# Cross-attention and expert FFN on one core: set-up reordered, last pair's sums ahead of the gathers, rows spread by transposes

## What is computed

```python
x = x + xattn(layernorm(x), ctx, q_w, k_w, norm_w, gate_w, gate_b)   # 16 sequences of 128 tokens, 256 wide
x = x + ffn(layernorm(x), combine_weights, top_idx, W1, b1, W2, b2)  # 8 experts, 512 rows each

def xattn(h, mem):
    n = rmsnorm(h) * norm_w
    v = concat(n, mem)
    a = softmax(mask((n @ q_w.T) @ (v @ k_w.T).T / 16))
    g = sigmoid(h @ gate_w.T + gate_b)
    return (1 - g) * h + g * (a @ v)

def ffn(x):       # expert e: rows tok = top_idx[:, e]
    y = gelu(x[tok] @ W1[e] + b1[e]) @ W2[e] + b2[e]
    out[tok] += y * combine_weights[tok, e]
```

## Time and profile before

| | us |
|---|---|
| median of 3 runs (275.99 to 277.49) | 276.33 |
| the profiled execution | 277.63 |
| its span, first to last instruction | 275.8 |
| PE, DVE, ACT, POOL busy, share of the span | 96%, 79%, 68%, 57% |

### The profile page before, as it was taken

The page is one execution under the profiler, slowest core; times in us unless marked ns, Lnnn a source line. Parts: engine busy times, 40 slices in busy tenths (PEclk is TensorE's granted clock), DMA queues, the critical chain, the costliest instruction groups (busy, mean ns, idle before and its releaser), DMA issues.

```text
span 275.8 us, 5127 instructions
## 1 busy us (share of the span) xinstructions
PE 265.7 (96%) x1474; PEld 226.7 (82%) x1474; DVE 219.0 (79%) x554; ACT 188.2 (68%) x349; POOL 155.9 (57%) x153
## 2 busy tenths in 40 slices
PE   6999999999989999999999999999999999999992
PEld 2688899999866888888888888888888888888992
DVE  1788999898986499968878896796887889689452
ACT  2488898887575976685677587658657758763540
POOL 4283865655843956556446466655645646605515
PEclk9799999999999999999999999999999999999998
DMA  7993247568454956455565544546555461201211
GB/s 219 358 263 94 77 123 218 155 214 276 114 182 123 350 160 157 124 192 167 138 195 163 154 139 135 157 122 209 156 138 189 156 175 53 67 26 47 62 38 69
DMA packets 30292, 42.44 MB, mean 154 GB/s; under 512 B 5251, under 2 KB 24015, under 8 KB 30148
## 3 DMA queue, kind: packets, MB, share of 16 engines
q1 hardware_dynamic: 25392, 30.00, 34.4%
q0 software_dynamic: 4608, 12.24, 15.4%
q10 hardware_dynamic: 276, 0.00, 0.1%
HBM read 33.54 MB, written 9.24 MB: 155 GB/s over the span
## 4 chain that ended last, share of the span: by engine, by line
PE 83%; DVE 6%; issue 4%; POOL 3%; ACT 2%; DMA 1%; DVEq 0%; POOLq 0%; ACTq 0%
PE bank L1398 19%; PE bank L1185 13%; PE bank L1186 12%; PE bank L1187 12%; PE bank L1399 10%; PE bank L1229 4%; PE bank L1274 3%; PE bank L1326 2%; PE bank L1345 1%; PE bank L1349 1%; PE bank L1346 1%; DMA x_all<-in_x_dram 1%; PE bank L1181 1%; POOL out_dram L552 1%; PE bank L1258 1%
## 5 line engine op out<-in xcount | busy, mean ns | idle before, releaser
L742 ACT ACTIVATE keysT<-bank,biasT 128x512 f32<-128x512 f32 x63 | 43.7, 693 | 55.6 <-PE bank L1187 41.8
L552 POOL DMA_INDIRECT out_dram<-h,sidx x32 | 36.8, 1151 | 41.9 <-DVE h L1077 37.0
L543 POOL DMA_INDIRECT x_all<-out_dram,idx_all x32 | 35.4, 1106 | 23.9 <-DMA out_dram<-h,sidx 16.5
L1185 PE MATMUL bank<-x_hi,w_parts 128*128 128x512 f32 (+1 forms) x114 | 45.1, 396 | 0.0
L1186 PE MATMUL bank<-x_lo,w_parts 128*128 128x512 f32 (+1 forms) x114 | 44.4, 389 | 0.0
L1187 PE MATMUL bank<-x_hi,w_parts 128*128 128x512 f32 (+1 forms) x114 | 44.1, 387 | 0.0
L1102 DVE TENSOR_TENSOR g_lo<-keysT,g_hi 128x512 fp32r<-128x512 f32 x32 | 22.1, 690 | 24.9 <-ACT g_hi L743 23.4
L1398 PE MATMUL bank<-w_parts,g_hi 128*128 128x512 f32 x112 | 40.5, 396 | 0.0
L539 POOL DMA_INDIRECT x_all<-token_rows,idx_all x28 | 29.0, 1036 | 19.4 <-DVE factor L1126 7.7
L1107 DVE TENSOR_TENSOR w_parts<-w_raw,w_parts 128x512 fp32r<-128x512 f32 x56 | 38.9, 696 | 0.0
L748 ACT CAST w_parts<-w_raw 128x512 fp32r<-128x512 f32 x56 | 34.9, 623 | 0.0
(11 more groups left out here) (186 smaller groups left out, 685.9 us busy)
## 6 DMA issues: line engine op xcount, KB each, us to landing
w_raw<-in_L_ffn_W_dram SPq DMA_DIRECT2D x32, 512.0 KB
idx_rows<-in_L_ffn_top_idx_dram SPq DMA_DIRECT2D x8, 256.0 KB, 4.0
out_dram<-x SPq DMA_DIRECT2D x8, 256.0 KB, 3.0
hn_cnat<-in_ctx_dram SPq DMA_DIRECT2D x7, 256.0 KB, 2.7
token_rows<-xn SPq DMA_DIRECT2D x7, 256.0 KB, 2.2
hn_cnat<-in_L_ffn_b_dram SPq DMA_DIRECT2D x1, 1024.0 KB, 6.9
x_all<-in_x_dram SPq DMA_DIRECT2D x3, 256.0 KB, 4.4
x_all<-in_x_dram SPq DMA_DIRECT2D x1, 768.0 KB, 8.1
```

Source lines behind the costliest of these rows:

```text
L543: g.indirect_dma_start(accg[:, t, :], None, flat, list_of(e, t)).then_inc(acc_in[t], 16)
L552: g.indirect_dma_start(flat, idx(sidx[:, t:t + 1].bitcast(U32), 0), newrow[:, t, :], None, bounds_check=N - 1, oob_is_err=False).then_inc( ...
L742: a.activation(g32[:, f % NG, :], ps_up[f % 2][:, :], ACT.Gelu_apprx_tanh, bias=bias)
L1185: t_.matmul(dst, lhs_hi, rhs_hi, start=first, stop=False)
```

## The change

- Set-up: k_w is loaded from ACT's queue at its head; norm_w and gate_b both by partition, spread over the partitions by four transposes of a broadcast column. M_rows(1) goes ahead of the first pair's transposes, the context transposes ahead of the query product, and ACT and DVE follow that order. One more matmul on zeros. DVE moves the statistics of sequences 6 to 9 in part behind the first mask and behind the first gate.
- Expert 0's chunks 2 and 3 are loaded behind pair 2's context.
- Pair 7: POOL adds x + h ahead of all gathers; three gathers follow, then 1/std of pair 6, then the fourth gather. PE transposes the probabilities ahead of the first late rows and takes the parts in another order; DVE makes the low part of b = 0 ahead of pair 7's second shift.
- The seen table is filled as pairs (half the elements) ahead of expert 1's gathers. The last list's load goes behind pair 7's stores.
- Expert 7: f = 4 moves into `last_downs`; the last expert's scatters wait without an instruction between.

```diff
...
             load_weight(0, q_w, wts_in)
-            load_weight(1, k_w, wts_in)
             load_x(1, 2, 4)
...
-            for c in range(NCH):
-                sp.dma_start(w_chunk_dst(c), w_chunk(0, c)).then_inc(w_in[c], 16)
...
+            for c in range(2):
+                load_chunk(0, c)
...
             load_ctx(2)
+            for c in range(2, NCH):
+                load_chunk(0, c)
...
                         sp.dma_start(rows_v[:, 2 * r + b, 0:H], xn_last[:, b, :]).then_inc(xn_out[r % 2], 16)
+                    sp.wait_ge(onehot_rdy, NB - EARLY)
+                    load_lists(IDX_PARTS - 1)
                 elif r < EARLY_PAIRS:
...
                             .then_inc(xn_out[late % 2], 16)
-                    sp.wait_ge(onehot_rdy, NB - EARLY)
-                    load_lists(IDX_PARTS - 1)
...
                 if is_last(p):
-                    gather_first_rows(range(1, NT))
+                    gather_first_rows(range(NT - 1))
                 if not is_last(p):
...
                     rstd(p - 1, 1 - s)
-                if p == LAST - 1:
-                    gather_first_rows(range(1))
+                if is_last(p):
+                    gather_first_rows(range(NT - 1, NT))
 
...
                     pool.wait_ge(new_rdy, NT * e + t + 1)
-                    take_waits(pool)
+                    if not is_last(e):
+                        take_waits(pool)
                     g.indirect_dma_start(flat, idx(sidx[:, t:t + 1].bitcast(U32), 0), newrow[:, t, :], None,
...
 
-            for s in range(2):
-                pool.wait_ge(xn_out[s], 16 * (NPAIR // 2) + 16 + 16 * s)
-                pool.wait_ge(x2_out[s], 16 * (NPAIR // 2) + 16)
-            gather_rows(1, 1)
             pool.wait_ge(pv_mm, NPAIR)
-            g.memset(seen, 1.0).then_inc(consts, 1)
+            pool.wait_ge(last_xn[1], 1)
+            g.memset(seen_pairs, ONE_ONE).then_inc(consts, 1)
             pool.wait_ge(consts, 4)
...
                                 pattern=[[1, C]], channel_multiplier=-NT).then_inc(seen_rdy, 1)
+            for s in range(2):
+                pool.wait_ge(xn_out[s], 16 * (NPAIR // 2) + 16 + 16 * s)
+                pool.wait_ge(x2_out[s], 16 * (NPAIR // 2) + 16)
+            gather_rows(1, 1)
...
             a = nc.scalar
-            act.dma_start(norm_wT[:, :], norm_w.rearrange("(k p) -> p k", p=P), allow_slow_non_contiguous=True)\
+            act.dma_start(wts[:, 1, :, :], k_w.rearrange("(k p) h -> p k h", p=P)).then_inc(wts_in, 16)
+            act.dma_start(norm_wT, norm_w.rearrange("(k p) -> p k", p=P), allow_slow_non_contiguous=True)\
                 .then_inc(nwT_in, 16)
-            act.dma_start(vec_rows[:, 0:H], norm_w.rearrange("(a h) -> a h", a=1)).then_inc(vec_in, 16)
-            act.dma_start(vec_rows[:, H:2 * H], gate_b.rearrange("(a h) -> a h", a=1)).then_inc(vec_in, 16)
+            act.dma_start(norm_w_gate_bT[:, 1, :], gate_b.rearrange("(k p) -> p k", p=P),
+                          allow_slow_non_contiguous=True).then_inc(gate_b_in, 16)
...
                     normed_transposed(2, 0)
-                    for c in range(NCH):
+                    for c in range(2):
+                        act.wait_ge(w_in[c], 16)
+                elif not isinstance(p, int) and s == 0:
+                    for c in range(2, NCH):
                         act.wait_ge(w_in[c], 16)
...
             M_high(0)
-            hn_transposed(0, 0)
             M_high(1)
+            hn_transposed(0, 0)
+            context_transposed(0, 0)
             act.wait_ge(hnT_lo_rdy, 1)
...
             query(0)
-            context_transposed(0, 0)
             hn_rows(1, 1)
...
                 dve.wait_ge(x_steps, steps[0])
-                v.tensor_scalar(neg_mean[:, b0:b1_], mv[:, b0:b1_, 0], -1.0, None, ALU.mult)
+                if b0:
+                    v.tensor_scalar(neg_mean[:, b0:b1_], mv[:, b0:b1_, 0], -1.0, None, ALU.mult)
...
             M_low(0)
-            x_sums(3, 4, 1)
+            M_low(1)
             hnT_low(0, 0)
+            x_sums(3, 4, 1)
             x_aggregates(2, 4)
-            M_low(1)
             x_variances(2, 4)
...
             x_rms(0, 4, 2)
-            x_stats(6, 10, 3)
-            x_variances(6, 10)
+            x_sums(6, 8, 3)
             dve.wait_ge(ident_rdy, 2)
...
                     v.tensor_copy(idx_f[:, :], idx_all[:, :, :].rearrange("p t e -> p (t e)")).then_inc(idx_rdy, 1)
+                    x_sums(8, 10, 3)
                     hnT_low(1, 1)
...
                 if is_first(p):
+                    x_aggregates(6, 10)
+                    x_variances(6, 10)
...
+
+            def last_pair_low(b):
                 dve.wait_ge(late_hi_rdy, 3 + b)
...
 
+            last_pair_low(0)
+            last_pair_shift(1)
+            dve.wait_ge(shift_rdy, NPAIR + 1)
+            v.tensor_scalar(xn_last[:, 1, :], x2[:, last_s, 1, :], rstd2[:, last_s, 1:2], shift2[:, last_s, 1:2],
+                            ALU.mult, ALU.add).then_inc(last_xn[1], 1)
+            last_pair_low(1)
+
...
-            keep_warm(9)
+            keep_warm(10)
...
             M_rows(0)
-            hn_transposes(0, 0)
             M_rows(1)
-            pe.wait_ge(vec_in, 32)
-            pe.wait_ge(ones_rdy, 1)
-            t_.matmul(banks[7][:, :], ones_row[:, :], vec_rows[:, :], start=True, stop=True).then_inc(bc_mm, 1)
+            hn_transposes(0, 0)
+            pe.wait_ge(nwT_in, 16)
+            pe.wait_ge(gate_b_in, 16)
+            for n in range(2):
+                for k in range(KH):
+                    last = t_.transpose(banks[7][:, (n * KH + k) * P:(n * KH + k + 1) * P],
+                                        norm_w_gate_bT[:, n, k:k + 1].broadcast_to([P, P]), ident[:, :])
+            last.then_inc(bc_mm, 1)
+            context_transposes(0, 0, 0)
             pe.wait_ge(setup_lo, 2)
             query(0, 0)
-            context_transposes(0, 0, 0)
             pe.wait_ge(gatew_in, 16)
...
                         .then_inc(setup_mm, 1)
-                    pe.wait_ge(log_rdy, 2 * NPAIR - 1)
-                    pe.wait_ge(late_hi_rdy, 1)
-                    for b in range(2):
-                        late_rows(0, b, late_hi, first=b == 0)
                 pe.wait_ge(exp_rdy, 2 * p + 2)
...
                 if is_last(p):
-                    early_rows(range(1))
+                    pe.wait_ge(log_rdy, 2 * NPAIR - 1)
+                    pe.wait_ge(late_hi_rdy, 1)
+                    for b in range(2):
+                        late_rows(0, b, late_hi, first=b == 0)
                 pe.wait_ge(pT_ev, p + 1)
...
             each_pair(pe, attention)
-            early_rows(range(1, NT))
-            for n in range(2):
...
+            early_rows(range(1))
+            pe.wait_ge(late_lo_rdy, 1)
+            for b in range(2):
+                late_rows(0, b, late_lo)
+            early_rows(range(1, NT - 1))
+            pe.wait_ge(late_hi_rdy, 2)
+            for b in range(2):
+                late_rows(1, b, late_hi)
+            early_rows(range(NT - 1, NT))
+            pe.wait_ge(late_hi_rdy, 3)
+            late_rows(2, 0, late_hi)
+            pe.wait_ge(late_lo_rdy, 2)
...
             for k in range(KH):
+                cols = slice(k * P, (k + 1) * P)
+                pe.wait_ge(late_hi_rdy, 4)
+                t_.matmul(ps_xT[k][:, :], late_hi[2][:, 1, cols], onehot[:, 5, :], start=False, stop=False)
...
                 for t in range(NT):
-                    for f in range(NF - 3, NF):
+                    for f in range(NF - 4, NF):
                         if f < NF - 1:
...
                     up(e, s, f)
-                    if not (is_last(e) and f == NF - 1):
+                    if not (is_last(e) and f >= NF - 2):
                         down(e, s, f - 2)
```

56 lines of the change are left out of this document (24 added, 32 removed).

## The result

The changed kernel's median is 274.74 us (6 runs, 274.39 to 275.33). The kernel before has 276.91 in the same comparison; one of its six runs (280.45) was in a slower state, the median of the others is 276.33, and ratios are of fast runs: 0.993, 95% interval [0.9905, 0.9955]. So the changed kernel is faster, by 0.7%, and 2.1 us slower than forecast: above the 274.5 that all upper ends gave, just inside the 274.8 of the rivals. The profiled execution took 275.01, with a span of 273.2 against 275.8: 2.6 us where the sum had 3.7.

A forecast was written before the change was run, and what follows sets the result against it. It took PE as the bound nearly throughout from 15 us, with DVE binding in pair 7. Set-up -1.9, into expert 0 -1.2 and the end -0.6 sum to -3.7 us: median 276.33 becomes 272.6, range 271.5 to 274.5 (all upper ends).

The forecast's parts named there:

- the sum against 277.63, and take the same difference off the median: Whole kernel: -3.7 us summed on the profiled 277.63 gives 273.9; the same off the median 276.33 gives 272.6.
- Set-up, forecast -1.9: Start to first gate: query product 9.85 instead of 11.86, first mask 2.5 us ahead, 0.6 lost; range -1.0 to -2.5.
- M_rows at 5.35: Set-up on PE: k_w issued earlier from a second queue lets M_rows(0) start at 5.35 instead of 5.91, range 5.2 to 5.9.
- The loss behind the first gate, forecast 0.6: Set-up, behind the first gate: moved DVE statistics and POOL's later powers give back 0.6 us of the mask's 2.5.
- the slower rival: Set-up: gate_b, loaded element by element, lands late and stalls PE's spread; each us costs one; chance 0.05, 0.02 above 276.33.
- Into expert 0, forecast -1.2: Pair 7 to expert 0: x + h off DVE's mix and a new order of late rows; range -0.5 to -1.4 us.
- The 0.84 of x + h: Pair 6's mix: DVE stood still 0.84 us beside POOL's x + h; starting that earlier gains all of it.
- The fourth gather: Into expert 0: lands at 80.15, PE wants it at about 80.4, no cost; a rival with 81.2 had 0.06.
- The end, forecast -0.6: Expert 7 and last scatters: first scatter 0.8 us earlier, PE then the bound, last scatter 272.5; range -0.3 to -0.9.
- the dropped instruction: The last scatters at the end: dropping it was counted only within the 0.9 us end of that term's range.
- Little of the set-up arrives: Rival, 15 to 32 us: DVE and POOL take the set-up's gain, leaving 0.6 of it; median 273.9, chance 0.12.
- k_w from ACT gains nothing: Rival, set-up: queues share the DMA engines, first x lands the full 0.75 us late; median 273.0, chance 0.09.

The follow-up runs named there:

- b1: Kernel before with only k_w loaded from ACT's queue, ahead of norm_w: 276.27 us, ratio 0.9996 to the kernel before.
- a3: Changed kernel with gate_b's 4-byte pieces loaded behind the second context load, its spread behind the gate weight's transposes: 274.57 us, ratio 0.9930 to the kernel before.
- e4: Changed kernel with DVE's statistics of sequences 6 to 9 back ahead of the first mask: 275.14 us, ratio 0.9945 to the kernel before.
- a4: Changed kernel with POOL's first x + h and normed rows ahead of the late powers: 274.75 us, ratio 0.9925 to the kernel before.
- e1: Changed kernel with pair 1's x + h ahead of the last powers on POOL: 275.17 us, ratio 0.9947 to the kernel before.
- a2: Changed kernel with norm_w and gate_b loaded as contiguous rows, spread by a matmul with a row of ones: 274.35 us, ratio 0.9917 to the kernel before.
- a1: Changed kernel with k_w back on SP's queue behind q_w: 276.31 us, ratio 0.9981 to the kernel before.

## Why the prediction was wrong

- **The step that failed first** is "the sum against 277.63, and take the same difference off the median". In the profiled execution the clock falls, and it took 1.5 us longer than the two others profiled, in which it doesn't; the median of 276.33 lies 0.2 above these two. The 1.3 us between profile and median stood in the text as a number to carry along; they were the price of the fall. The changed kernel's profile lies only 0.27 above its median. Of the 2.1 us that the forecast missed, 1.0 are this step, and 1.1 are terms of the sum by the first profile: 0.7 in the set-up, 0.4 into expert 0, 0.1 at the end. What the change saves by keeping the clock up can't be taken off an execution that never lost it. The Trainium skill, "TensorE: Matmul & The Clock Gate", section What's actually happening, says that the gate's window runs free of the kernel's start; the text used that for the changed kernel only. The three profiles of the kernel before agree with it.
- **Set-up, forecast -1.9.** Against the first profile -1.24, against the others 0.0 (30.37 and 30.40; 30.66 and 30.14). The forecast had the changed kernel itself nearly right, pair 2's logits at 30.0; the base was wrong, since the profile with the fall has these logits 1.5 us later than the two others. Mis-sized in it: M_rows at 5.35 was 6.02 and 5.93. The text let it wait for k_w alone, and it waited for q_w, which landed 4.7 us after its issue instead of 3.9 (4.5 in b1 with k_w's bytes beside it, 4.3 in a3 without gate_b's pieces). x's second load, not named at all, made DVE wait 0.89 in the first profile and not in the second. First mask, forecast 13.6: 14.20 and 13.68. The loss behind the first gate, forecast 0.6, was 0.65, by POOL's late powers as said.
- **Pieces.** gate_b element by element was seen as a wait of PE's (0.48 us; the slower rival). That it takes half or more of every other load's rate was not. The Trainium skill, "DMA: Bandwidth & Descriptors", section Why small descriptors are slow (HBM only), has a fixed cost of each packet. The traces agree in that pieces of 4 bytes cost far more than their bytes; what share of the dip that cost makes, they don't tell.
- **Into expert 0, forecast -1.2**: -0.81 in the first profile, -1.1 in the second and in most variants. The 0.84 of x + h was right (0.75 less of the mix, and 0.75 to 1.1 net by undoing it). The other 0.36, from the order of the late rows, came where gather 0 was in time or nearly: x_hi starts 0.59 us behind the end of DVE's last low part instead of 0.96. In the first profile PE's backlog behind gather 0 took it (0.92). The fourth gather, which I watched, was in time; the first was not: from its end on POOL (72.90) to its rows on PE it took 3.8 us, where the text had read 2.1 for landing from the fourth.
- **The end, forecast -0.6**: 0.54, confirmed by undoing it (0.62). The last DVE row was forecast at 271.15 by the old times; expert 0's first gelu is 1.99 us earlier, and 269.16 + 1.99 is 271.15. To the 0.01 that is luck, since the stretch between the two marks wasn't forecast. That the dropped instruction was worth little (below 0.1) was not seen.
- **The rivals.** "Little of the set-up arrives" gives 273.9 and is the nearest of them; its mechanism, DVE and POOL between 15 and 32 us, is what e4, a4 and e1 show. That its number is the nearest is luck: the loss behind the first gate was the one that the sum already had, and what didn't arrive of the set-up was the fall's price. "k_w from ACT gains nothing" holds alone (0.9996), not beside the piecewise loads. The Trainium skill, "DMA: Bandwidth & Descriptors", section Issuing engines are not separate DMA queues, gave it; the run of that part alone agrees, with the first x 0.2 us late. What held, taken from 276.1, gives 274.8 by the first profile (0, 0.8 and 0.55 less) and 274.4 by the second (0.2, 1.2 and 0.3 less); measured 274.74 and 274.44. The late place of chunks 2 and 3, costed at 0, the tenth matmul on zeros and the halved table were not tried apart.

## What to carry to other kernels

Where a profiled execution is further from the median than the runs scatter, look first for what it has that the others don't (a fallen clock, a late gather), and profile again; a saving there counts only for the share of executions that pay. Loads in 4-byte pieces belong behind everything that someone waits for, though here that brought no more than 0.4 us. And where DVE and POOL share a stretch, moving a POOL row moves the hold to another DVE row: name that row before counting the gain.

## What was new of the hardware

- Loads of 1 KB in 256 pieces of 4 bytes took the rate of all queues down to 97 to 240 GB/s, where it is about 350 and more beside them: one such load for 0.7 to 2.1 us (a2 and a3), two together for 2.4 to 2.8 (a1 and the changed kernel).
- Three profiles of one kernel with waits of PE of 0.3 to 1.2 us at the same places: the clock fell to 0.50 at 8 to 11 us in one and stayed at 1.00 there in two.
- A DVE cast or tensor_scalar with a single SBUF operand, 6 to 32 elements wide, is held by a POOL sum or product until that ends (1.18, 1.26, 1.33 us for 0.17), while statistics run beside it at their usual 0.35 each. The Trainium skill, "SBUF — State Buffer", section Who interferes with whom, names cast and tensor_scalar among those that can take the shared ports; the traces agree.
- From the end of gather 0 on POOL to its rows on PE it took under 3.3 us in a2, 3.8 in the changed kernel's first profile and 4.1 in a4, at the same place of the queue; at such a distance it decides 0.3 us of the stage.
